# Two layers of attention and feed-forward on one core: where the second attention's weights are turned, and the heads' scale in two halves

## The reference

```
x = x + _L0_xattn_ref(_layernorm(x), ctx_1024, ctx_1024, igate_kernel, ..., outnorm_scale)
x = x + _L0_ffn_ref(_layernorm(x), w_gate, w_up, w_down)
x = x + _L1_xattn_ref(_layernorm(x), ctx_1024, ctx_1024, w_q, b_q, w_k, b_k, w_v, b_v, w_o, b_o)
x = x + _L1_ffn_ref(_layernorm(x), w_router, wi, wo)

# _L0_xattn_ref, 4 heads of 64
log_fg = jax.nn.log_sigmoid(fg);  cs = jnp.cumsum(log_fg, axis=2)
D = jnp.exp(log_D - max_log_D)                 # log_D: cs - cs' + ig, lower triangle
C = (qk / 8) * D
normalizer = jnp.maximum(jnp.abs(jnp.sum(C, axis=-1)), jnp.exp(-max_log_D))
h = (C / (normalizer + EPS)) @ vh
h_norm = (h - mean) * rsqrt(var + 1e-05) * outnorm_scale     # per head
```

## Time and profile before

| what | value |
|---|---|
| median of 3 runs | 599.63 us (599.15 to 603.48) |
| profiled execution, its own time | 599.1 us |
| its span in the trace | 597.4 us |
| PE busy | 515.9 us (86%) |
| DVE busy | 376.1 us (63%) |
| ACT busy | 321.7 us (54%) |
| POOL busy | 141.2 us (24%) |
| mean granted clock of PE | 0.948 of full |

### The profile page before, as it was taken

One profiled execution on the slowest core, in us unless ns is written; L12 is line 12 of the kernel. 1 busy time (PEld: TensorE's weight loads), 2 busy tenths in 40 slices (PEclk: granted clock), 3 DMA queues, 4 the chain that ended last, 5 costly groups with the idle time before them and its releaser, 6 DMA issues.

```text
span 597.4 us, 9314 instructions
## 1 busy us (share of the span) xinstructions
PE 515.9 (86%) x3283; PEld 364.4 (61%) x3283; DVE 376.1 (63%) x948; ACT 321.7 (54%) x672; POOL 141.2 (24%) x202
## 2 busy tenths in 40 slices
PE   1979989899999701899989999995799999999994
PEld 1558856654444201787657787874667776777673
DVE  6576689845489989779678699987403432143101
ACT  2846658723489969771298899984222112211220
POOL 2005634000000000000323223111234344434431
PEclk9979999999999955999999999999699999999998
DMA  7910000000000000035000101015133536453410
GB/s 219 277 45 1 3 1 1 2 0 1 0 0 1 1 0 1 0 103 179 2 1 1 37 2 37 1 38 176 28 110 120 183 122 204 119 182 120 133 44 22
DMA packets 31994, 37.58 MB, mean 63 GB/s; under 512 B 8656, under 2 KB 27728, under 8 KB 31952
## 3 DMA queue, kind: packets, MB, share of 16 engines
q1 hardware_dynamic: 28880, 29.07, 15.0%
q0 software_dynamic: 3072, 7.95, 4.5%
HBM read 30.14 MB, written 6.88 MB: 62 GB/s over the span
## 4 chain that ended last, share of the span: by engine, by line
PE 72%; DVE 13%; ACT 9%; DMA 2%; issue 2%; POOL 1%; SPq 0%; POOLq 0%; DVEq 0%
PE pA L2056 12%; PE pB L2074 9%; PE pC L1725 6%; PE pC L1764 5%; PE pA L1758 3%; PE pB L1774 3%; PE pA L1680 2%; PE pC L1588 2%; PE pC L1680 2%; PE pB L1680 2%; ACT XIT L708 2%; PE pC L2067 2%; DVE am L1181 2%; PE pC L1634 2%; PE pB L1854 2%
## 5 line engine op out<-in xcount | busy, mean ns | idle before, releaser
L478 POOL TENSOR_TENSOR arena<-KT,par 128x256 f32<-128x256 f32 x32 | 18.9, 613 | 248.4 <-DVE XIT L1255 186.5
L2056 PE MATMUL pA<-arena 128*128 128x320 f32 x256 | 74.1, 438 | 0.4 <-ACT arena L884 0.4
L896 ACT ACTIVATE arena<-pA 128x320 f32<-128x320 f32 x64 | 28.0, 437 | 71.8 <-PE pA L2056 71.2
L2074 PE MATMUL pB<-arena 128*128 128x256 f32 x256 | 59.3, 385 | 0.0
L2056 PEld LDWEIGHTS pA<-arena 128*128 128x128 f32 x256 | 47.4, 190 | 18.9 <-issue 1.1
L2074 PEld LDWEIGHTS pB<-arena 128*128 128x128 f32 x256 | 47.4, 190 | 9.4 <-issue 3.1
L1147 DVE TENSOR_REDUCE am<-arena 128x1 f32<-128x512 f32 x48 | 32.1, 682 | 23.0 <-ACT arena L648 22.9
L1725 PE MATMUL pC<-wdnT,XIT 128*128 128x256 f32 x192 | 42.9, 381 | 1.8 <-DVE XIT L1255 1.8
L1331 DVE TENSOR_REDUCE rm<-pA 128x16 f32<-128x2048 f32 x16 | 36.7, 2292 | 8.7 <-PE pA L1758 8.7
L1725 PEld LDWEIGHTS pC<-wdnT,XIT 128*128 128x128 f32 x192 | 36.0, 190 | 7.9 <-DVE XIT L1255 2.8
L1764 PE MATMUL pC<-ident,arena 128*128 128x128 f32 x240 | 35.4, 280 | 1.5 <-ACT XIT L744 0.8
(11 more groups left out here) (342 smaller groups left out, 1154.5 us busy)
## 6 DMA issues: line engine op xcount, KB each, us to landing
arena<-in_L_ffn_wi SPq DMA_DIRECT2D x8, 1024.0 KB, 6.0
arena<-in_L_ffn_wo SPq DMA_DIRECT2D x8, 1024.0 KB
X<-in_x SPq DMA_DIRECT2D x4, 512.0 KB, 5.8
arena<-in_ctx SPq DMA_DIRECT2D x4, 512.0 KB, 7.5
out<-X SPq DMA_DIRECT2D x4, 512.0 KB, 3.0
token_rows<-arena SPq DMA_DIRECT2D x4, 512.0 KB, 5.9
arena<-in_L_ffn_w_up SPq DMA_DIRECT2D x1, 768.0 KB, 7.5
arena<-in_L_ffn_w_gate SPq DMA_DIRECT2D x1, 768.0 KB, 9.2
```

The lines of the kernel that those rows point to most:

```text
L896: nc.scalar.activation(HT[:, u, f, :], ps[2 + f % 2][:, 0:ROWS], ACT.Relu).then_inc(s["h_relu"], 1)
L2056: last = mm(ps[2 + f % 2][:, 0:ROWS], WI[:, u, k, f * P:(f + 1) * P], XET[:, u, k, :], start=(k == 0), stop=(k == KD - 1))
L2074: last = mm(ps[4 + c][:, 0:D], HT[:, u, f, c * P:(c + 1) * P], WO[:, u, f, :], start=(f == 0), stop=(f == NFT - 1))
```

## The change

- SP's transfers: the second attention's k, v, q and o weights are issued directly behind the feed-forward's three, ahead of six small ones (`oscale` to `wrt`) that stood before them; o was first of the four and is last.
- `W_ORDER` begins with k, v, q, o. All four are turned within the forget chain, on PE between its steps: k and v ahead of L1555's product, half of q behind it, half of q and half of o behind the first transpose, half of o behind the second. ACT copies the four out between L579 and L581. The first spread of maxima then waits for the fourth copy. Behind the first attention PE goes to `keys_values(0)` at once; the wait for all of `u_copied` is in front of its first value product.
- The heads' scale is made in two halves of 32 heads. The first half's normalizers, spreads and variances are put at the end of turns 5, 6 and 7 of DVE's loop, its inverse roots (`head_scale(0)`) in turn 8, ahead of the statistics of blocks 14 and 15. The second half follows the loop; ACT's part of it (`rsqrt(3)`) stands behind `head_norm(3)`.
- ACT normalizes all four heads of blocks 0 to 7 (56 of 64 heads, where it was 48), DVE the fourth head only of blocks 8 to 15. `keys(1)` stands behind block 7 (was 9), `keys(2)` behind 13 (was behind 15); DVE's `values_kept` in steps 1, 8 and 14. DVE adds block t in step t, where it was block t - 2.
- Beside the sixteen turned blocks stand nine weight pieces, where it was eleven.

The diff, cut to its core (numbers in calls such as `rsqrt(4, 8)` to `rsqrt(5, 8)` that only count on are left out):

```diff
-        W_ORDER = (10, 11, 0, 1, 2, 3, 4, 5, 6, 7, 8, 9, 12)
+        W_ORDER = (10, 11, 9, 12, 0, 1, 2, 3, 4, 5, 6, 7, 8)
+
+        TURN_BESIDE = (0, 2, 4, 5, 7, 8, 10, 11, 13)
+
+        HB = NB // 2
...
+            for n, nme in ((1, "k"), (2, "v"), (0, "q")):
+                sp.dma_start(LN[:, n], A[f"L1_xattn_w_{nme}"].rearrange("(k p) d -> p k d", p=P)).then_inc(s[f"w{nme}_in"], 16)
+
+            for k in range(KD):
+                for e in range(2):
+                    sp.dma_start(LN[:, 3, k, :].rearrange("p (j e x) -> p j e x", j=4, e=2)[:, :, e],
+                                 A["L1_xattn_w_o"].rearrange("(k p) (e j x) -> k p e j x", p=P, e=2, j=4)[k, :, e]).then_inc(s["wo_in"], 16)
             late(oscale[:, :], A["L0_xattn_outnorm_scale"])
             late(bv[:, :], A["L1_xattn_b_v"])
             late(bo[:, :], A["L1_xattn_b_o"])
             sp.dma_start(bk[:, :], A["L1_xattn_b_k"].rearrange("(k p) -> p k", p=P), allow_slow_non_contiguous=True).then_inc(s["late_in"], 16)
             sp.dma_start(bq[:, :], A["L1_xattn_b_q"].rearrange("(k p) -> p k", p=P), allow_slow_non_contiguous=True).then_inc(s["late_in"], 16)
             sp.dma_start(wrt[:, :, :], A["L1_ffn_w_router"].rearrange("(k p) e -> p k e", p=P)).then_inc(s["late_in"], 16)
-            for k in range(KD):
-                for e in range(2):
-                    sp.dma_start(LN[:, 3, k, :].rearrange("p (j e x) -> p j e x", j=4, e=2)[:, :, e],
-                                 A["L1_xattn_w_o"].rearrange("(k p) (e j x) -> k p e j x", p=P, e=2, j=4)[k, :, e]).then_inc(s["wo_in"], 16)
-            for n, nme in ((1, "k"), (2, "v"), (0, "q")):
-                sp.dma_start(LN[:, n], A[f"L1_xattn_w_{nme}"].rearrange("(k p) d -> p k d", p=P)).then_inc(s[f"w{nme}_in"], 16)
...
                 pool.wait_ge(s["h_normed"], b + 1)
-                pool.wait_ge(s["last_normed"], b + 1)
+                if b >= HB:
+                    pool.wait_ge(s["last_normed"], b - HB + 1)
...
+            def first_weights_copy(i):
+                n = W_ORDER[i]
+                act.wait_ge(s["wtr_done"], i + 1)
+                nc.scalar.activation(wT[n - 9], ps[2 + i % 2][:, :].rearrange("p (k c) -> p k c", k=2), ACT.Copy).then_inc(s["wtr_copied"], 1)
+            for i in range(4):
+                first_weights_copy(i)
...
-            for i in range(2):
-                n = W_ORDER[i]
-                act.wait_ge(s["wtr_done"], i + 1)
-                nc.scalar.activation(wT[n - 9], ps[2 + i % 2][:, :].rearrange("p (k c) -> p k c", k=2), ACT.Copy).then_inc(s["wtr_copied"], 1)
-            rsqrt(2, NB * NH0)
-            act.wait_ge(s["head_stat"], 1)
-
-
-            def head_norm(b, u, h):
-                for n in range(NH0 - 1):
+            rsqrt(2, HB * NH0)
+
+            def head_norm(b):
+                act.wait_ge(s["head_stat"], 1 + b // HB)
+                for n in range(NH0 if b < HB else NH0 - 1):
                     last = nc.scalar.activation(at(HU, b)[:, n, 0:DH0], at(HU, b)[:, n, 0:DH0], ACT.Identity, scale=rstd[:, cols(b * NH0 + n, 1)], bias=s2[:, cols(b * NH0 + n, 1)])
                 last.then_inc(s["h_normed"], 1)
...
-                head_norm(b, b % 2, b // 2)
+                head_norm(b)
                 if b == 3:
+                    rsqrt(3, HB * NH0, HB * NH0)
                     keys(0)
-                if b == 9:
+                if b == 7:
                     keys(1)
-            keys(2)
-            rsqrt(3, NB)
+                if b == 13:
+                    keys(2)
+            rsqrt(4, NB)
             keys(3)
             def copy_x(b):
@@ -641,8 +645,8 @@
                 nc.scalar.activation(XITv[:, :, b * P:(b + 1) * P], ps[b % 2][:, 0:2 * P].rearrange("p (k n) -> p k n", k=2), ACT.Copy).then_inc(s["xit_ready"], 1)
             for b in range(NB):
                 copy_x(b)
-                if b % 3 != 2:
-                    weights_copy(2 + b - b // 3)
+                if b in TURN_BESIDE:
+                    weights_copy(4 + TURN_BESIDE.index(b))
...
+            def denominators(h):
+                if h == 0:
+                    dve.wait_ge(s["fgate_act"], 2)
+                rows = slice(h * HB, (h + 1) * HB)
+                d = [den[:, n, half[h]].rearrange("p (b h) -> p b h", h=NH0) for n in range(2)]
+                rowsum = HU[:, rows, :, DH0]
+                link(V_.scalar_tensor_tensor(out=d[0], in0=rowsum, scalar=-1.0, in1=rowsum, op0=ALU.mult, op1=ALU.max))
+                link(V_.tensor_tensor(d[1], d[0], nm[:, rows, :], ALU.max))
+                link(V_.tensor_scalar(d[0], d[1], 1e-6, None, ALU.add))
+                link(V_.reciprocal(d[1], d[0]))
+
+            def head_scale(h):
+                inverse_roots(2 + h, HB * NH0, den[:, 1, half[h]], h * HB * NH0)
+                V_.scalar_tensor_tensor(out=s2[:, half[h]], in0=mean[:, half[h]], scalar=-1.0, in1=rstd[:, half[h]], op0=ALU.mult, op1=ALU.mult).then_inc(s["head_stat"], 1)
...
+                if t == NB // 2:
+                    head_scale(0)
                 for b in (2 * t - 2, 2 * t - 1):
                     if b >= 0:
                         head_stats(b, 0, 0)
+                if t == 5:
+                    denominators(0)
+                if t == 6:
+                    spreads(HB * NH0, DH0, den[:, 1, half[0]])
+                if t == 7:
+                    variance(HB * NH0, den[:, 1, half[0]])
+            denominators(1)
+            variances(HB * NH0, DH0, den[:, 1, half[1]], HB * NH0)
+            head_scale(1)
...
-            for t in range(NB + 3):
+            for t in range(NB + 1):
+                if HB <= t + 2 < NB:
+                    last_head(t + 2, 0, 0)
                 if t < NB:
-                    last_head(t, t % 2, 0)
-                if 2 <= t < NB + 2:
-                    add_heads(t - 2, 0, 0)
-                if 3 <= t:
-                    stats2(t - 3, 0, 0)
-                if t in (4, 10, 16):
-                    values_kept(t // 6)
+                    add_heads(t, 0, 0)
+                if t >= 1:
+                    stats2(t - 1, 0, 0)
+                if t in (1, 8, 14):
+                    values_kept((1, 8, 14).index(t))
             dve.wait_ge(s["row_stats"], NB)
-            moments(3, NB, D)
+            moments(4, NB, D)
...
+            weights_turn(0)
+            weights_turn(1)
             pe.wait_ge(s["fgate_dve"], 2)
             mm(ps[7][:, 256:256 + NB * NH0], tri[:, :], lf[:, :, :].rearrange("p b h -> p (b h)"), start=True, stop=True).then_inc(s["fgate_pe"], 1)
+            weights_turn(2, (0,))
             pe.wait_ge(s["fgate_dve"], 3)
             tr(ps[7][0:NB * NH0, 0:P], Acol[:, :, :].rearrange("p b h -> p (b h)"), ident[:, :]).then_inc(s["fgate_pe"], 1)
+            weights_turn(2, (1,))
+            weights_turn(3, (0,))
             pe.wait_ge(s["fgate_dve"], 4)
             tr(ps[7][:, P:P + NB * NH0], mT[:, :], ident[0:NB * NH0, 0:NB * NH0]).then_inc(s["fgate_pe"], 1)
+            weights_turn(3, (1,))
...
-                    pe.wait_ge(s["ct_ready"], NB // 2)
+                    pe.wait_ge(s["wtr_copied"], 4)
...
+                    elif i == 0:
+                        pe.wait_ge(s["u_copied"], NB)
...
-            weights_turn(0)
-            weights_turn(1)
-            pe.wait_ge(s["wtr_copied"], 2)
-            pe.wait_ge(s["u_copied"], NB)
             for c in range(4):
                 keys_values(c)
```

91 lines of the change are left out of this document (43 added, 48 removed).

## The result

The kernel with the change takes 603.63 us (median of 20 runs, 600.10 to 605.92); the kernel before, in the same session, 599.89 us (20 runs, 599.03 to 603.48). The ratio is 1.0048, with a 95% interval of 1.0033 to 1.0063. The prediction was 598.4 us with a range of 596.0 to 601.2: wrong in sign and outside its range. The profiled execution took 603.28 us, with a span of 601.2 (before: 599.1 and 597.4). Of the 34 executions of the kernel before beside e9 to e12, 18 took 598.5 to 600.1 us and 16 took 601.3 to 603.1, so its median falls between two groups, and its trace is one of the lower.

The account below looks back on a forecast made before the run. It took PE to bound the attention, its first turn at half clock, then PE beside DVE and ACT. Terms -2.2 + 1.0 = -1.2 us on the 599.63 us median gave 598.4 us, range 596.0 to 601.2.

Parts of the forecast that it names:

- the earlier heads: Behind the first attention: ACT starts its heads at 76.5 instead of 81.90, 5.35 us earlier, 4.45 of it used by added work.
- Transfers: Ahead of the forget chain: moved weights arrive before they are wanted, cost nothing, covered by 2 us of margin.
- the forecast 0.15: End of the forget chain: the first spread waits for ACT's copy of the last weight and starts 0.15 us later.
- Forget chain and clock, -2.2: Forget chain into the first attention: added transposes keep PE's clock full, so the third spread comes 2.2 us earlier.
- Rival C: Forget chain: the clock falls all the same, +0.5 + 1.0 = +1.5 us, 601.1 us; chance 0.17.
- Broken up, not full: Forget chain: doubt that PE, at most two thirds busy from 30 to 33 us, would keep its clock.
- Inserted pieces, 0: DVE's attention loop: three pieces of some 1.0 us each fit into 1.34 us of waiting per turn, costing nothing.
- The sign of error: First attention's loop: turns 5 to 7 longer than 4.4 us would show the prediction wrong.
- Rival D: Heads' scale: DVE and POOL operations meet at the upper bound, +1.4 us, 599.8 us; chance 0.15.
- PE's wait for group 1, 2.9: Second value group: PE waits 2.9 us for values_kept(0), loses its clock, and the products take 5.2 us instead of 3.5.
- The later waits: Later value products: PE waits 1.0 us for values_kept(1) and again 1.0 us for values_kept(2).
- L1660 1.0 us later: Turning of the maximum: DVE ends last, so L1660 starts 1.0 us later than 118.12, without the forget chain's shift.

Follow-up runs that it names:

- e9: The kernel before, with identity transposes into a free bank filling PE's idle time in the forget chain, nothing else: 600.06 us, ratio 0.9981.
- e12: The changed kernel run once more, unchanged: 602.42 us, ratio 1.0034.
- e1: The kernel before plus the change's transfers, turned weights and direct keys, with the heads' scale left whole: 601.62 us, ratio 1.0023.
- e3: The changed kernel with the first half's three pieces together in turn 8 instead of in turns 5 to 7: 607.17 us, ratio 1.0111.
- e8: The changed kernel plus four identity transposes behind each of turned blocks 3, 6, 9, 12, 14 and 15: 604.82 us, ratio 1.0092.
- e6: The changed kernel with DVE's values_kept(0) ahead of head_scale(1) instead of behind the first statistic: 604.88 us, ratio 1.0086.
- e5: The changed kernel with POOL's two weight products of blocks 9 to 15 cut to one of nine parts, weights left unscaled: 600.54 us, ratio 1.0002.
- e7: As e6, against the changed kernel, with values_kept(1) and (2) also moved to DVE's steps 4 and 9 from 8 and 14: 600.28 us, ratio 0.9990.
- e11: e10 plus four identity transposes behind each of turned blocks 3, 6, 9, 12, 14 and 15: 597.57 us, ratio 0.9938.
- e4: The changed kernel with ten calls' worth of identity products ahead of PE's wait for group 1: 602.63 us, ratio 1.0055.
- e10: e7 plus 7, 1, 3 and 4 identity transposes at the four waits of the forget chain: 597.89 us, ratio 0.9959.
- e2: The changed kernel with transfers, W_ORDER and turned weights as before, leaving the scale in halves alone: 602.6 us, ratio 1.0038.

## Why the prediction was wrong, point by point

The forecast was -1.2 us; the profiled execution showed +3.8 in the span (and 0.4 outside it). The difference of 5.0 us lies in these terms: 0.4 in the forget chain, 0.8 in the loop, 0.4 up to the first head, 1.9 from there to the turn of the maximum, 1.5 behind it. Two steps failed: the inserted work and the scale beside POOL, put at nothing, and the price of the clock behind PE's wait and behind the maximum. In the second execution (e12, span 598.9, +1.5) the clock part is small: 1.1 us by the first spread, most of it ahead of the chain, 0.8 in the loop, 0.4 to the first head, 0.6 to the maximum, nothing behind it.

- **Transfers:** the weights cost nothing, as said; no spread waited for one. The first spread, released at 35.47 by ACT's fourth copy as forecast, was late by 0.3 us beyond the forecast 0.15; 0.18 of that lies ahead of the chain, the rest in the chain itself.
- **Forget chain and clock, -2.2:** right in this execution (-1.8 at the third spread), wrong as a property of the kernel. The same chain was traced in nine executions (after, e1, e3 to e8, e12). The clock was full in three, at half in both windows or nearly so in three (e1, e3, e6), and lost for a part in three (e5, e7, e8). Rival C, which I gave 0.17, is as frequent in them as my forecast. The kernel before also has its better executions: filling its chain gained 1.1 us in the ratio, not 2.3. So -2.2 was the wrong size for a median even where the mechanism was right. "Broken up, not full" was the right doubt; e9 to e11, where it is almost filled (in e9 the longest wait left is 0.40 us), kept the clock.
- **Inserted pieces, 0:** wrong, an error of reading. "0.2 us each, 0.3 us to spare" took prices from places where POOL is idle. In the loop POOL works 2.6 of 4.4 us, and two operations of each piece then take 0.57 to 0.71 us, so a piece takes 1.7 to 2.0 us where the sum had 1.0. The loop lost 0.8 of the 1.8 us. The sign of error that the prediction named for it, turns over 4.4 us, did not come: the loss is in PE's one wait at the end. The first head came 0.4 us later than summed (4.5 against 4.1 from the last value product). The meeting costs 1.2 us there (e5 has 3.3), half in turn 7's piece and half in the roots (L939, L940); the sum was 0.8 too long without it, which hid part. Rival D had the meeting only in the scale that follows the loop, with a chance of 0.15; e5 shows that it is in both, 2.0 us in all.
- **PE's wait for group 1, 2.9:** right who waits for whom; the size (2.92, twice) owes something to luck, since the sum had no meeting in it and e5, without the meeting, waits 1.69. Its price was mis-sized: the sixteen products were reckoned at 5.2 us, as in the earlier trace rows, and took 6.71 and 5.41. The earlier trace rows was one draw too. From the first head to the turn of the maximum the sum had 42.6 us; the two executions show 44.5 and 43.2, e4 and e5 with the clock kept 41.5 (B less the way to the first head, which is 4.5, in e5 3.3).
- **The later waits** of 1.0 us at groups 2 and 3: right (1.05 and 1.06). The mechanism of this part was right down to who waits for whom.
- **The turning, "L1660 1.0 us later":** that was to be without the forget chain's gain. L1660's counterpart L1695 came 2.3 us later with 1.0 us already gained ahead of it, so B grew by 3.3; the reasons are the points on the pieces and on PE's wait.
- **Behind the maximum:** not in the sum at all. It was 1.5 us in one execution and nothing in the other. The clock was lost there in after, e1, e3 and e4 and partly in e6, and full in the nine others, in e5, e7, e10 and e12 with nine weight pieces and nothing added beside them. e12 even has the very instructions of after. So the smaller number of pieces doesn't decide it alone. That it makes the loss more frequent is not excluded (five of nine such executions lost it, none of the three with eleven: before, e2, e9); what decides it stays open.

In the median the change costs about 2.9 us (ratio 1.0048) or 2.0 (e12). What is shown of it: a ring of waits, worth 3.7 to 5.0 us of stretch B by e7 with the clock that it loses, and POOL's and DVE's meeting, worth 2.0 us by e5. Against it stand the earlier heads and, in some executions, the clock. The ring in one sentence: PE's group 1 waits for `values_kept(0)`, which stands behind `head_scale(1)`, which waits for ACT's roots behind block 3; ACT's `keys(1)` behind block 7 waits for PE's group 1; and DVE's next `values_kept` stands behind block 8, which waits for `keys(1)`. The prediction had every link of it and summed the waits. It forecast -1.2 since it put the meeting at nothing, took the clock's cost behind the wait from one draw, and had no clock term behind the maximum; as a forecast of the median it also credited the kept clock in full. These parts overlap (the later first head is a part of the ring's wait), so they do not add up to the median's 2.0 to 2.9 us.

## What to carry to other kernels

A gain that consists of a kept clock is a gain of some executions. Reckon it at its mean, or fill the idle time wholly, as e10 does. When work is put into the idle time of DVE, look at what POOL does in that very stretch, and take the price from a row beside it. Before work is moved earlier on one strand, write down for each buffer who gives it back and what that engine waits for ahead of it: giving three pairs of banks back earlier (e7) took 3.7 to 5.0 us off a stretch that the change had made 2.0 to 3.3 us longer.
